# State-space powers from TensorE products with a table of exponents, in a four-stage transformer kernel on one core

## What is computed

```python
dt = jnp.exp(log_dt)
A = -jnp.exp(A_re_log) + 1j * A_im
dtA = A * dt[:, None]                               # 128 channels x 32 modes
C = (C_re + 1j * C_im) * (jnp.expm1(dtA) / A)
K = 2.0 * jnp.einsum('hn,hnl->hl', C, jnp.exp(dtA[:, :, None] * l)).real
y = irfft(rfft(z, n=2*L) * rfft(K, n=2*L), n=2*L)[..., :L] + z * D_skip[:, None]
out = jnp.einsum('oh,bhl->bol', W, gelu(y)) + bvec[None, :, None]
return out[:, :Hh] * jax.nn.sigmoid(out[:, Hh:])    # z is the layer norm of h; h = h + this
```

## Time and profile before

| | us |
|---|---|
| median of 3 runs | 1387.14 (1383.18 to 1394.52) |
| the profiled execution, its own time | 1394.2 |
| its span, first to last instruction | 1392.4 |
| PE busy in the span | 939.7 (67%) |
| DVE busy | 936.1 (67%) |
| POOL busy | 508.0 (36%) |
| ACT busy | 482.8 (35%) |

### The profile page before, as it was taken

The page is one execution under the profiler, slowest core; times in us unless marked ns, Lnnn a source line. Parts: engine busy times, 40 slices in busy tenths (PEclk is TensorE's granted clock), DMA queues, the critical chain, the costliest instruction groups (busy, mean ns, idle before and its releaser), DMA issues.

```text
span 1392.4 us, 19437 instructions
## 1 busy us (share of the span) xinstructions
PE 939.7 (67%) x7176; PEld 625.3 (45%) x7176; DVE 936.1 (67%) x1586; ACT 482.8 (35%) x1204; POOL 508.0 (36%) x384
## 2 busy tenths in 40 slices
PE   4052262262273617999999967759889788979877
PEld 4032042141042306787878743324466443546543
DVE  5999899799785663464645468968855346955443
ACT  3133043043031422121212141016677334768622
POOL 4862832832710360000000032437934133954310
PEclk9575685685685758999999978979989779979968
DMA  1151071071071418454544040000011200012100
GB/s 59 40 92 32 3 130 32 2 129 30 0 129 30 183 44 146 91 91 90 90 90 90 0 147 0 0 0 0 16 46 49 80 24 25 1 31 62 32 0 30
DMA packets 60445, 75.52 MB, mean 54 GB/s; under 512 B 37544, under 2 KB 42036, under 8 KB 58676
## 3 DMA queue, kind: packets, MB, share of 16 engines
q1 hardware_dynamic: 60376, 74.60, 24.5%
HBM read 52.11 MB, written 1.51 MB: 39 GB/s over the span
## 4 chain that ended last, share of the span: by engine, by line
PE 39%; DVE 29%; POOL 13%; issue 10%; ACT 5%; DMA 2%; SPq 0%; DVEq 0%; POOLq 0%; ACTq 0%
PE bank L960 6%; PE bank L962 6%; PE bank L961 6%; POOL rest L1190 3%; ACT rest L1143 3%; POOL rest L1180 3%; PE bank L1378 2%; POOL rest L1186 2%; PE bank L641 2%; DVE kept L379 2%; DVE main L534 2%; PE bank L1387 2%; DVE rest L453 2%; PE bank L1445 2%; PE bank L1446 2%
## 5 line engine op out<-in xcount | busy, mean ns | idle before, releaser
L406 POOL TENSOR_TENSOR kept<-kept 128x8 f32<-128x8 f32 x20 | 4.0, 201 | 456.9 <-DVE kept L383 456.9
L1143 ACT ACTIVATE rest<-bank,main 128x128 f32<-128x128 f32 x256 | 113.4, 479 | 12.4 <-POOL main L1201 10.8
L641 PE MATMUL bank<-main,rest 128*128 128x512 f32 x64 | 38.6, 759 | 92.3 <-DVE main L573 86.5
L807 ACT ACTIVATE x_high<-main 128x512 fp32r<-128x512 f32 x48 | 30.3, 633 | 199.1 <-DVE main L881 199.1
L960 PE MATMUL bank<-x_high,w_low 128*128 128x512 f32 x192 | 76.7, 399 | 20.4 <-DVE x_low L886 20.4
L629 PE MATMUL bank<-main 128*32 128x64 f32 x1024 | 22.4, 270 | 99.2 <-DMA main<-main 98.8
L1209 POOL TENSOR_TENSOR rest<-rest,main 128x512 f32<-128x512 f32 x64 | 65.4, 1043 | 47.3 <-DVE main L1274 47.3
L420 ACT ACTIVATE main<-bank,kept 128x128 f32<-128x128 f32 x40 | 14.5, 469 | 185.7 <-POOL kept L413 185.7
L881 DVE TENSOR_TENSOR main<-kept,rest 128x512 f32<-128x512 f32 x48 | 33.0, 690 | 68.1 <-PE bank L962 43.7
L961 PE MATMUL bank<-x_low,w_high 128*128 128x512 f32 x192 | 76.2, 397 | 0.0
L960 PE MATMUL bank<-hid_high,w_low 128*128 128x512 f32 x192 | 75.6, 394 | 0.7 <-DVE main L905 0.7
(11 more groups left out here) (283 smaller groups left out, 2873.1 us busy)
## 6 DMA issues: line engine op xcount, KB each, us to landing
rest<-share_d SPq DMA_DIRECT2D x4, 3072.0 KB, 21.4
rest<-share_d SPq DMA_DIRECT2D x4, 2304.0 KB, 20.3
main<-main SPq DMA_DIRECT2D x32, 256.0 KB, 5.1
main<-k_pad SPq DMA_DIRECT2D x16, 512.0 KB, 7.4
rest<-main SPq DMA_DIRECT2D x32, 256.0 KB, 3.4
main<-w_dram SPq DMA_DIRECT2D x2, 3072.0 KB, 14.5
main<-main SPq DMA_DIRECT2D x32, 128.0 KB, 2.3
rest<-tables_dram SPq DMA_DIRECT2D x2, 2048.0 KB, 9.2
```

The source lines that it names most:

```text
L641: last = T.matmul(bank[4 + 2 * (b % 2) + k][:, :], w_out[:, k * P:(k + 1) * P], rhs, start=True, stop=True)
L1143: last = A.activation(probs[:, p, 4 * r + m, :], bank[2 * p + r][:, m * P:(m + 1) * P], ACT.Exp, scale=row_scale[:, c, r, m:m + 1], bias=r ...
```

## The change

- **Exponents as a table.** `expo` holds, for both halves of 64 partitions, a block-diagonal matrix of 32 x (64 + 32) columns with 64 near exponents and 32 of whole chunks (768 KB, read once). dtA is transposed (`s4_pe_dta`), and products with the table give the turns and the real exponents of all 64 powers at once in PSUM (`s4_pe_near_angles`, `s4_pe_far_angles`, `s4_pe_exponents`; 4, 2 and 4 products of 512 columns).
- **Sines of all powers.** ScalarE rounds the turns (`s4_act_round_near`, `_far`), VectorE subtracts (`s4_dve_near_turns`, `s4_dve_far_turns`, reading PSUM), ScalarE takes sines of 128x2048 into `pow_im` and `pow_re`, and the exponential in place in PSUM. VectorE multiplies by it: two operations on 128x2048. The low-high anchors, `k_re` and `k_im` and all of `s4_pool_powers`' 128x2048 operations are gone; g and the decay stay on GpSimd (`s4_pool_phases`), the decay behind `s4_u_re`.
- **Coefficients in the selector.** `sel_re`, `sel_im` (128x128 each) hold coefficient times selector, and TensorE makes the kernel rows by 64 products of 64 columns with 4 columns of weights, and 8 small ones for the skip. ScalarE copies them by 4 + 4 operations; four DMAs in place of one write them out.
- **Layers written out.** The four layers are Python loops on every engine; `phi`, `g`, `r_chunk` have two buffers; the semaphores "turn" in this stage are gone, and a few others are merged.

```diff
 def exponents():
-    e = [LOW - 1 - b for b in range(LOW)] + [LOW * (HIGH - 1 - a) for a in range(HIGH)] + [CHUNK * c for c in range(CHUNKS)]
-    return np.array(e, np.float32)
+    near, far = CHUNK - 1 - np.arange(CHUNK), CHUNK * np.arange(CHUNKS)
+    rows = [np.kron(np.eye(HG), e) for e in (near, far)]
+    return np.tile(np.concatenate(rows, axis=1), (2, 1)).astype(np.float32).reshape(-1)
...
-            V.tensor_copy(s0, theta[:, :, ONE])
-            V.tensor_tensor(anc_re, mag, cosn[:, :, 0:NEAR], ALU.mult)
-            V.tensor_tensor(anc_im, mag, sn[:, :, 0:NEAR], ALU.mult).then_inc(sem("s4_anchors"), 1)
+            V.tensor_copy(s0, pow_re[:, :, FIRST])
+            link(V.tensor_copy(mag1, mag[:, :, FIRST]))
+            V.tensor_tensor(pow_im, pow_im, mag, ALU.mult).then_inc(sem("s4_pow_im"), 1)
+            V.scalar_tensor_tensor(pow_re, pow_re, 1.0, mag, ALU.subtract, ALU.mult, reverse0=True).then_inc(sem("s4_pow_re"), 1)
...
-            V.tensor_tensor(four(pow_re), hi(anc_re), lo(anc_re), ALU.mult)
-            link(V.tensor_tensor(four(k_re), hi(anc_im), lo(anc_im), ALU.mult))
-            V.tensor_tensor(pow_re, pow_re, k_re, ALU.subtract).then_inc(sem("s4_pow_re"), 1)
-            dve.wait_ge(sem("s4_pow_re"), G + 1)
-            V.tensor_tensor(k_re, pow_re, c2_re.unsqueeze(2).to_broadcast([P, HG, CHUNK]), ALU.mult).then_inc(sem("s4_k_re"), 1)
+            V.tensor_tensor(sel_re, sel[:, 0, :].unsqueeze(1).to_broadcast(wide), c2_re.unsqueeze(2).to_broadcast(wide), ALU.mult)
+            V.tensor_tensor(sel_im, sel[:, 1, :].unsqueeze(1).to_broadcast(wide), c2_im.unsqueeze(2).to_broadcast(wide), ALU.mult).then_inc(sem("s4_sel"), 1)
...
             if more:
-                s4_dve_reduce(dve, chain, L + 1)
+                s4_dve_near_turns(dve, L + 1)
...
             link(V.tensor_tensor(b_im, b_im, s_b, ALU.subtract))
+            if more:
+                s4_dve_far_turns(dve, L + 1)
...
-            pe.wait_ge(sem("s4_k_re"), L + 1)
-            pe.wait_ge(sem("s4_k_im"), L + 1)
-            for k in range(PIECES):
-                T.matmul(bank[4 + k][0:GROUPS, :], sel[:, 0, :], k_re[:, PIECE * k:PIECE * (k + 1), :], start=True, stop=False)
-                T.matmul(bank[4 + k][0:GROUPS, :], sel[:, 1, :], k_im[:, PIECE * k:PIECE * (k + 1), :], start=False, stop=True).then_inc(sem("s4_k_ps"), 1)
+            pe.wait_ge(sem("s4_sel"), L + 1)
+            for hh in range(HG):
+                q, at = hh // PIECE, CHUNK * (hh % PIECE)
+                dst = bank[4][32 * q:32 * q + GROUPS, at:at + CHUNK]
+                T.matmul(dst, sel_re[:, hh, :], pow_re[:, hh, :], start=True, stop=False)
+                last = T.matmul(dst, sel_im[:, hh, :], pow_im[:, hh, :], start=False, stop=True)
+            last.then_inc(sem("s4_k_ps"), 1)
...
             pe.wait_ge(sem("s4_back"), (L + 1) * (HG // 2))
+            if more:
+                s4_pe_near_angles(pe, L + 1)
             pe.wait_ge(sem("s4_z"), L + 1)
...
+            if more:
+                s4_pe_far_angles(pe, L + 1)
+                pe.wait_ge(sem("s4_in"), L + 1)
+                s4_pe_exponents(pe, L + 1, 0)
...
             if more:
-                act.wait_ge(sem("s4_phases"), L + 1)
-                s4_act_decay(act, L + 1)
-            if more:
-                s4_act_sines(act, L + 1, CLOSE, "s4_sin")
+                s4_act_round_near(act, L + 1)
+                s4_act_sines_near(act, L + 1)
+                s4_act_round_far(act, L + 1)
+                s4_act_sines_far(act, L + 1)
+                s4_act_magnitudes(act, L + 1, LOW_BANKS)
             act.wait_ge(sem("s4_u"), L + 1)
...
+        def s4_pool_phases(pool, chain, G):
+            pool.wait_ge(sem("s4_mag"), G * 2 + 1)
+            if G:
+                pool.wait_ge(sem("s4_u_re"), G)
+            G_.tensor_tensor(decay[:, :, 1:CHUNKS], r_chunk[G % 2].unsqueeze(2).to_broadcast([P, HG, CHUNKS - 1]),
+                             ones.unsqueeze(1).to_broadcast([P, HG, CHUNKS - 1]), ALU.mult)
+            pool.wait_ge(sem("s4_sin_far"), G * 3 + 3)
+            pool.wait_ge(sem("s4_coef"), G + 1)
...
-            s4_act_magnitudes(act, 0)
-            s4_act_decay(act, 0)
+            s4_act_rates(act, 0)
...
+            s4_act_dtaT(act, 0)
+            s4_act_round_near(act, 0)
+            s4_act_round_far(act, 0)
+            s4_act_magnitudes(act, 0, HIGH_BANKS)
             act.wait_ge(sem("mod_ready"), 1)
```

More of the change, by code:

```diff
@@ L369, in ln_pe_back @@
                     c = 4 * b + t
-                    last = nc.tensor.transpose(bank[4 + b][:, t * P:(t + 1) * P], normed[:, c, :], ident)
+                    last = nc.tensor.transpose(bank[first + b][:, t * P:(t + 1) * P], normed[:, c, :], ident)
                 last.then_inc(sem("ln_back"), 1)
@@ L580, in s4_dve_layer, with s4_pe_dta, s4_pe_near_angles @@
                 V.tensor_tensor(hT[:, sl], hT[:, sl], glu_sig[:, sl], ALU.add).then_inc(sem("s4_h"), 1)
-        def s4_pe_layer(pe, L, first):
+        def s4_pe_dta(pe, G):
+            pe.wait_ge(sem("s4_dta"), G + 1)
+            nc.tensor.transpose(bank[6][0:2 * HG, 0:P], dta.rearrange("p a h -> p (a h)"), ident).then_inc(sem("s4_dtaT_ps"), 1)
+        def s4_pe_near_angles(pe, G):
+            pe.wait_ge(sem("s4_dtaT"), G + 1)
+            for k in range(4):
+                last = nc.tensor.matmul(bank[4 + k][:, :], dtaT[HG:2 * HG], expo[HG:2 * HG, 512 * k:512 * k + 512], start=True, stop=True)
+            last.then_inc(sem("s4_x_ps"), 1)
@@ new lines, in s4_pe_far_angles, with s4_pe_exponents @@
+        def s4_pe_far_angles(pe, G):
+            pe.wait_ge(sem("s4_turns"), G * 2 + 1)
+            for k in range(2):
+                at = NEAR_COLS + 512 * k
+                last = nc.tensor.matmul(bank[4 + k][:, :], dtaT[HG:2 * HG], expo[HG:2 * HG, at:at + 512], start=True, stop=True)
+            last.then_inc(sem("s4_x_ps"), 1)
+        def s4_pe_exponents(pe, G, first):
+            for k in range(4):
+                last = nc.tensor.matmul(bank[first + k][:, :], dtaT[0:HG], expo[0:HG, 512 * k:512 * k + 512], start=True, stop=True)
+            last.then_inc(sem("s4_x_ps"), 1)
@@ new lines, in s4_pe_layer @@
+            for hh in range(HG):
[4 more added lines that the diff above has]
+            last.then_inc(sem("s4_k_ps"), 1)
+            pe.wait_ge(sem("s4_layer_in"), L * 64 + 64)
+            for q in range(PIECES):
+                dst, hs = bank[5][32 * q:32 * q + GROUPS, 0:PIECE], slice(PIECE * q, PIECE * (q + 1))
+                T.matmul(dst, sel[:, 0, :], small[8][:, hs], start=True, stop=False)
+                last = T.matmul(dst, ident[0:GROUPS, 0:GROUPS], skip[:, hs], start=False, stop=True)
@@ L1620, in _ @@
             dve.wait_ge(sem("mod_ready"), 1)
-            ln_dve(dve, LN_A, z_tok, hT, one_plus[:, 1:2], mod[:, 0:1])
-            s4_dve_reduce(dve, chain, 0)
+            s4_dve_near_turns(dve, 0)
+            s4_dve_far_turns(dve, 0)
+            ln_dve(dve, LN_A, z_tok, hT, one_plus[:, 1:2], mod[:, 0:1], first=0)
             dve.wait_ge(sem("s4_zero_out"), 16)
-            s4_dve_powers(dve, chain, 0)
-            with dve.Fori(0, S4_LAYERS - 1) as L:
-                chain.body(L, S4_DVE_LINKS)
-                s4_dve_layer(dve, chain, L, more=True)
-            chain.leave(S4_LAYERS - 1)
-            s4_dve_layer(dve, chain, S4_LAYERS - 1, more=False)
+            s4_dve_powers(dve, chain, 0, near(HIGH_BANKS))
+            for L in range(S4_LAYERS):
+                s4_dve_layer(dve, chain, L, more=L < S4_LAYERS - 1)
             dve.wait_ge(sem("s4_h"), S4_LAYERS * BLOCKS)
@@ L1651, in _ @@
             ln_pe_tokens(pe, xT)
+            pe.wait_ge(sem("consts_in"), 64)
+            s4_pe_dta(pe, 0)
+            pe.wait_ge(sem("expo_in"), 16)
             pe.wait_ge(sem("mod_ready"), 1)
-            ln_pe_back(pe, LN_A, z_tok)
-            pe.wait_ge(sem("consts_in"), 64)
-            s4_pe_layer(pe, 0, first=True)
-            with pe.Fori(1, S4_LAYERS) as L:
-                s4_pe_layer(pe, L, first=False)
+            s4_pe_near_angles(pe, 0)
+            s4_pe_far_angles(pe, 0)
+            pe.wait_ge(sem("s4_turns"), 2)
+            s4_pe_exponents(pe, 0, 4)
+            ln_pe_back(pe, LN_A, z_tok, first=0)
+            for L in range(S4_LAYERS):
+                s4_pe_layer(pe, L, first=L == 0, more=L < S4_LAYERS - 1)
             moe_pe(pe)
```

341 lines of the change are left out of this document (160 added, 181 removed).

## The result

| | before | after |
|---|---|---|
| median, us | 1386.3 (4 runs, 1383.18 to 1394.52) | 1321.85 (4 runs, 1319.02 to 1325.82) |
| ratio, 95% interval | | 0.9528 (0.9479 to 0.9577) |
| span of the profiled execution | 1392.4 | 1324.0 |
| last transpose of y starts | 444.19 | 378.04 |
| VectorE busy | 936.1 | 819.0 |

The change gains 64.5 us by the medians and 68.4 by the profiled spans; the forecast was 74. Inside the state-space block the gain is 66.2. So single executions differ by up to 16 us in a part that nobody edited, and the block's own end in the trace is the finer measure.

A forecast was written before the change was run, and what follows sets the result against it. VectorE's powers were taken to burden the state-space block, the first 460 us; TensorE bounds from 560 us on. Gains of 29 (layer 0), 45 (two layers) and 0 sum to 74 us off the median: 1313 us, range 1299 to 1339.

The forecast's parts named there:

- VectorE in front: Layer 2 before `zu`: L444 goes (0.83 us), L526 falls from 7.44 to 2.50; `zu` ready at 302.3, not 308.1.
- TensorE in front: Layer 2: kernel rows at 60 ns a record (7.7 us), copies, transposes, near angles (3.4); state products start 3.2 us earlier.
- Rival 1: Front moves to TensorE: a pair of small load and product costs 117 ns instead of 60; 1337 us, chance 0.2.
- From L642 to L541: Stretch behind the start of the state products: 7.86 us instead of 9.14, as in the last layer before.
- Written-out layers: Writing the layers out as Python loops costs 0 us, between -1 and +3.
- Last layer: No powers and no near angles there, L526 undisturbed already: no gain, with up to 1 us lost.
- To the end of `u`: Layer 2, next stretch: 18.6 us as before, plus 1.2 for far turns and 1.7 for GpSimd's decay.
- Powers: From `u` to the transpose of y: 12.2 us taken; transpose 22.6 us earlier in layer 2, 45 for two layers.
- Rival 3: ScalarE gets too late and the powers wait for it, past 5 us of cover; 1358 us, chance 0.03.
- Layer 0: First layer: transpose of y at 129.6 to 134.6, taken as 132, instead of 161.3; 29 us earlier.
- Rival 4: Slower through the clock: from 560 us on TensorE's granted clock falls to 0.80; 1411 us, chance 0.02.
- the powers cost: State-space block before: the powers cost some 29 us per layer, and VectorE pays them.

The follow-up runs named there:

- experiment 6: Kernel before with TensorE's layers written out and nothing else: 1385.7 us, ratio 1.0007; its other runs edited the changed kernel.
- experiment 1: Kernel before, with GpSimd's seven wide operations on the powers of layers 1 to 3 cut to one column: 1324.62 us, ratio 0.9575.

## Why the prediction was right or wrong

It said 1313 us, 1299 to 1339, and the time is 1321.85. The mechanism and each price on VectorE held; the missing 9 us lie mostly in TensorE's terms.

- **VectorE in front:** forecast `zu` 20.0 us behind the gate; measured in layer 2, 235.57 to 255.63, 20.1.
- **TensorE in front:** forecast 22.7 behind the gate. Layer 2: 22.6, and the kernel rows took 111 ns for a pair of records, so 55.7 each for the 60 taken, and 6.7 us in all for 7.7. That the whole came out right is in part luck: the rows were 1.0 shorter, and the near angles took 3.96 for 3.4. Rival 1 (117 ns) is out. So are, in this case, the 25 ns that the Trainium skill gives for up to 64 columns ("TensorE: Matmul & The Clock Gate", Back-to-back issue gap). Layer 1: 26.1, 3.4 late, all of it the lower granted level in the transposes and near angles. The sum took the full level for every layer; that is the first step that was mis-sized.
- **From L642 to L541:** forecast 7.9. Layer 1: 7.87. Layer 2: 10.1, last layer 9.9. "Written-out layers: 0, between -1 and +3" is the second mis-sized step. It holds in the kernel before (experiment 6), but in the changed one writing out cost the stop of 1.99 in layer 2, which the second pass of a loop does not have. The term asked only whether written-out products take their 7.05 us, not whether their instructions come in time beside the Toeplitz loads. Before, in layer 2 the products started at 308.19, and the loads ended by 309; a shorter front brings them together. The kernel before with a shorter front, the run of experiment 1, has a stop of 1.48 in the first pass of its loop. "Last layer: nothing" cost 2.0 for the same reason.
- **To the end of `u`:** forecast 21.5, measured 21.4 in layer 1, with the far turns at 1.22 and the decay's 1.7 as priced.
- **Powers:** forecast 12.2, measured 12.0. ScalarE's exponential ended 5.6 us before they began; the cover was put at 5. Rival 3 did not happen.
- **Layer 0:** forecast 129.6 to 134.6, taken 132, measured 134.15. All of the near angles (7.16) and exponents (7.19) ran at the lower level: its slow end.
- **Rival 4** (slower by the clock from 560 us on): the granted clock behind the block is 0.89 (0.88 before) and the part is not longer.

By layers the forecast gave 132, 81.4, 81.4 and 75; measured 134.15, 84.35, 82.6 and 76.95: short by 2.2, 3.0, 1.2 and 2.0, in sum 8.3. The block gained 66.2 against 74.

One thing the prediction said less clearly than the runs do: of the 29 us per layer that "the powers cost", some 19 were not VectorE's work but its waits. Taking GpSimd's operations away from beside them gives 60 of the 66 us.

## What to carry to other kernels

Before moving work off a busy VectorE, look whether its small operations last as long as GpSimd's beside them; if so, the busy time is waiting, and giving VectorE one operand in PSUM, or starting GpSimd's operation while VectorE reads PSUM, frees it with no work removed (one changed wait here: 5.1 us of the block). When a front gets shorter, list what it now runs beside: here big strided loads that held back TensorE's own instructions. In a dense stretch of small products, look at the instruction queue before you write a loop out: the second pass of a loop had no stops here. And in a kernel whose untouched part varies by 16 us between executions, judge small edits by the end of their own stage in the trace.
